# Softmax normalisation on ScalarE, and split condition blocks kept in DRAM, in a four-layer graph transformer

## The reference

```python
h = gcn(batchnorm(relu(layernorm(x))))
for i in range(4):
    q = ln(h, ln2_w[i], ln2_b[i]).reshape(16, 64, 512) @ Wq[i]     # 8 heads of 64
    k, v = cond @ Wk[i], cond @ Wv[i]                              # cond: (16, 256, 512)
    w = softmax(einsum('bnhd,bmhd->bhnm', q, k) * 64 ** -0.5)
    h = h + einsum('bhnm,bmhd->bnhd', w, v) @ Wo[i]
    u = ln(h, ln3_w[i], ln3_b[i]) @ geglu_w[i] + geglu_b[i]        # 512 -> 2 x 2048
    val, gate = split(u)
    h = h + (val * gelu(gate)) @ ffo_w[i] + ffo_b[i]
out = x + gcn(h) + relu(layernorm(x))
```

## Time and profile before

| | us |
|---|---|
| Time, median of 3 runs | 2686.38 (2684.01 to 2689.35) |
| The profiled execution's own time | 2677.4 |
| Its span, first to last instruction | 2675.6 |
| TensorE matmuls busy in it | 2401.6 (90%) |
| VectorE busy | 1936.9 (72%) |
| ScalarE busy | 1240.3 (46%) |
| GpSimd busy | 1419.8 (53%) |
| Mean granted TensorE clock | 0.962 of full speed |

### The profile page before, as it was taken

One profiled execution on the slowest core, in us unless ns is written; L12 is line 12 of the kernel. 1 busy time (PEld: TensorE's weight loads), 2 busy tenths in 40 slices (PEclk: granted clock), 3 DMA queues, 4 the chain that ended last, 5 costly groups with the idle time before them and its releaser, 6 DMA issues.

```text
span 2675.6 us, 39336 instructions
## 1 busy us (share of the span) xinstructions
PE 2401.6 (90%) x14270; PEld 2095.6 (78%) x14270; DVE 1936.9 (72%) x3287; ACT 1240.3 (46%) x2497; POOL 1419.8 (53%) x990
## 2 busy tenths in 40 slices
PE   7877888889997898889997988889997988889999
PEld 5356888878886888778886888877886888878887
DVE  9965888766566888866566888876656788876654
ACT  9933544553333545553333544553332544454322
POOL 3045765546554766546554756546555666546540
PEclk9898999999998999999998999999998999999999
DMA  2021000112111000112111000112110100112121
GB/s 71 1 112 38 33 32 32 33 40 64 55 58 41 32 33 24 40 40 63 56 62 38 33 32 17 40 32 71 56 59 32 45 20 32 40 32 71 55 96 62
DMA packets 87085, 122.29 MB, mean 46 GB/s; under 512 B 6321, under 2 KB 68401, under 8 KB 82033
## 3 DMA queue, kind: packets, MB, share of 16 engines
q1 hardware_dynamic: 86608, 115.60, 13.5%
q10 hardware_dynamic: 288, 4.19, 0.4%
HBM read 113.22 MB, written 6.55 MB: 45 GB/s over the span
## 4 chain that ended last, share of the span: by engine, by line
PE 54%; DVE 23%; POOL 8%; ACT 5%; issue 5%; DMA 4%; SPq 0%; DVEq 0%; POOLq 0%; ACTq 0%
PE ps L2265 7%; PE ps L2266 7%; PE ps L2267 7%; PE ps L2635 6%; PE ps L2639 6%; PE ps L2637 6%; PE ps L2512 3%; DMA stage<-in_condT 3%; PE ps L2515 3%; PE ps L2514 3%; DVE qbd L1945 2%; POOL cb L771 2%; POOL t_s L766 2%; DVE p_norm L1979 2%; DVE kv L1922 2%
## 5 line engine op out<-in xcount | busy, mean ns | idle before, releaser
L2512 PE MATMUL ps<-wv_hi,cb 128*128 128x256 f32 x896 | 265.4, 296 | 74.1 <-DVE kv L1907 50.7
L2512 PE MATMUL ps<-cb,wk_hi 128*128 128x256 f32 x896 | 265.1, 296 | 43.6 <-DVE kv L1922 20.1
L2514 PE MATMUL ps<-wv_lo,cb 128*128 128x256 f32 x896 | 258.6, 289 | 0.0
L2515 PE MATMUL ps<-wv_hi,cb 128*128 128x256 f32 x896 | 258.6, 289 | 0.0
L831 POOL TENSOR_TENSOR f_lo<-ff,f_hi 128x512 fp32r<-128x512 f32 x128 | 167.6, 1322 | 171.2 <-ACT f_hi L1420 171.0
L2514 PE MATMUL ps<-cb,wk_hi 128*128 128x256 f32 x896 | 258.1, 288 | 0.0
L771 POOL TENSOR_TENSOR cb<-stage,cb 128x512 fp32r<-128x512 f32 x160 | 218.2, 1375 | 74.9 <-ACT cb L980 74.9
L2515 PE MATMUL ps<-cb,wk_lo 128*128 128x256 f32 x896 | 257.4, 287 | 0.0
L2512 PEld LDWEIGHTS ps<-wv_hi,cb 128*128 128x128 f32 x896 | 177.0, 197 | 86.0 <-DVE kv L1907 56.4
L1979 DVE TENSOR_SCALAR p_norm<-p_exp,rinv 128x256 f32<-128x256 f32 x256 | 226.3, 924 | 4.7 <-DVE rinv L1976 0.2
L2200 DVE TENSOR_TENSOR h<-h,ps 128x512 f32<-128x512 f32 x256 | 169.9, 684 | 72.7 <-PE ps L2267 72.0
(11 more groups left out here) (363 smaller groups left out, 7497.5 us busy)
## 6 DMA issues: line engine op xcount, KB each, us to landing
stage<-in_pieces SPq DMA_DIRECT2D x256, 128.0 KB, 2.6
stage<-in_condT SPq DMA_DIRECT2D x32, 1024.0 KB, 4.9
stage<-in_pieces SPq DMA_DIRECT2D x44, 512.0 KB, 3.6
stage<-in_pieces SPq DMA_DIRECT2D x16, 256.0 KB, 3.2
at_s<-at_hi ACTq DMA_DIRECT2D x2, 2048.0 KB, 8.3
wq_raw<-in_pieces SPq DMA_DIRECT2D x8, 512.0 KB, 4.3
wo_raw<-in_pieces SPq DMA_DIRECT2D x8, 512.0 KB, 4.1
at_hi<-at_s SPq DMA_DIRECT2D x4, 1024.0 KB, 8.1
```

What stands on the lines that cost most here:

```text
L2512: pe.matmul(to, l_hi, r_hi, start=(fresh and i == 0 and k == 0), stop=False, skip_group_check=True)
L2514: pe.matmul(to, l_hi, r_lo, start=False, stop=False, skip_group_check=True)
L2515: last = pe.matmul(to, l_lo, r_hi, start=False, stop=(k == 1), skip_group_check=True)
```

## The change

It has four parts.

1. The two multiplications of a softmax unit move from DVE (`softmax`) to ACT (new `normalise`, an ACTIVATE with a scale per row). In the DVE queue the reciprocal moves too: behind the first `kv_late` in each unit, and ahead of `o_low`.
2. The seven split blocks of each group are made in layer 0 alone. SP writes each to DRAM (`cb_s`, 512 KB per block) as soon as its low part is done, and layers 1 to 3 load them back (`load_blocks`), a block at a time, each behind the value step that reads its predecessor in the same place. `cond_sum`, `cond_high` and `cond_low` are gone from layers 1 to 3. A KEYS step there waits for the DMA at j = 0 (four blocks) and j = 4 (three).
3. Openings: in layers 1 to 3 the weights Wv are loaded and split at the end of the layer before (loaded before the blocks, summed on DVE between the last `add_down`s). In layer 0 the raw blocks of group 0 get a place of their own, `raw0`, and are loaded earlier. `first_t2(1)` is cut in two halves around the last `q_product(0, .)`, and each transpose waits only for the copy of its own bank. `zero_q` and the splitting of q move.
4. POOL waits for the normalised tiles (`z2_ok`) ahead of the work that followed `first_rsqrt`: in the first half of the opening ahead of the splitting of Wq (and of blocks 4 to 6 in layer 0), in the second ahead of `zero_q`.

SP's loop over layers is written out in place of a loop on the engine. The core of the diff (the functions that only gained an argument `g` are left out):

```diff
@@ sync engine, start @@
-            sp.wait_ge(w_ok, 4)
-            load_raw(0)
+            sp.wait_ge(a_dec, NT)
+            sp.dma_start(flat(raw0[:, :, :]), condT[0].rearrange("p k n -> p (k n)")).then_inc(raw_in, 16)
...
+            for j in range(BLOCKS):
+                sp.wait_ge(c_lo, j + 1)
+                sp.dma_start(cb_s[0, j], cond_block_bits(j)).then_inc(cb_out, 16)
@@ sync engine, layer @@
+                def load_blocks(g, js, after):
+                    for j in js:
+                        if after is not None:
+                            sp.wait_ge(step_mm, after + j + 1)
+                        sp.dma_start(cond_block_bits(j), cb_s[g, j]).then_inc(cb_in[j // 4], 16)
...
-                with sp.Fori(2, GROUPS) as g:
-                    sp.wait_ge(c_lo, BLOCKS * GROUPS * l + BLOCKS * g)
-                    load_raw(g)
-                wait_apart(sp, c_lo, BLOCKS * GROUPS * l + BLOCKS * GROUPS)
+                if first:
+                    for g in range(1, GROUPS):
+                        for j in range(BLOCKS):
+                            sp.wait_ge(c_lo, BLOCKS * g + j + 1)
+                            sp.dma_start(cb_s[g, j], cond_block_bits(j)).then_inc(cb_out, 16)
+                        if g + 1 < GROUPS:
+                            load_raw(g + 1)
+                else:
+                    for g in range(1, GROUPS):
+                        load_blocks(g, range(BLOCKS), STEPS * kv_set(l, g - 1, VALUES))
...
                 if not last:
-                    load_raw(0)
+                    for k in range(2):
+                        sp.wait_ge(w_ok, FIRST_PIECES + PIECES * l + VALUE_PIECE[k] - 1)
+                        load_attn((pieces[base + 21], pieces[base + 25]), k, VALUE_PIECE[k] % 2)
                     wait_apart(sp, block_mm, 7 * (SETS - 1) * l + 7 * (SETS - 1))
+                    load_blocks(0, range(4), None)
                     load_whole(wq_raw, (pieces[base + 5], pieces[base + 9]))
-                    wait_apart(sp, c_lo, BLOCKS * GROUPS * l + BLOCKS * GROUPS + BLOCKS)
-                    for k in range(2):
-                        load_attn((pieces[base + 21], pieces[base + 25]), k, VALUE_PIECE[k] % 2)
+                    load_blocks(0, range(4, BLOCKS), None)
@@ gpsimd, opening of a layer @@
                 kv_low(l, 0, KEYS, 0)
                 first_rsqrt(2 * l + 1)
-                attn_low(VALUES, 0, l)
-                attn_low(VALUES, 1, l)
-                for n in range(3):
-                    cond_sum(GROUPS * l + 1, n)
+                pool.wait_ge(z2_ok, 2 * FIRST * l + 2 * FIRST)
+                if l == 0:
+                    pool.wait_ge(agg_mm, NT)
+                    pool.wait_ge(low_out, 32)
+                zero_q()
+                if l == 0:
+                    attn_low(VALUES, 0, 0)
@@ gpsimd, end of a layer @@
-                    for n in range(3):
-                        cond_sum(g, n)
-                    cond_low(g, 0)
-                    cond_sum(g, 3)
-                    for j in range(1, BLOCKS):
-                        cond_low(g, j)
+                    for k in range(2):
+                        attn_low(VALUES, k, l + 1)
                     first_rsqrt(2 * l + 2)
+                    pool.wait_ge(z2_ok, 2 * FIRST * l + 3 * FIRST)
                     for half in range(2):
                         wq_low(l + 1, half)
-                    zero_q()
@@ scalar engine @@
+                def normalise(u):
+                    act.wait_ge(rinv_ok, u + 1)
+                    for b in range(2):
+                        last = act.activation(pn[:, b, :], pe_[:, b, :], ACT.Identity, scale=rinv[:, b:b + 1])
+                    last.then_inc(pn_ok, 1)
@@ vector engine @@
                     dve.reciprocal(rinv[:, :], rsum[:, :]).then_inc(rinv_ok, 1)
-                    dve.wait_ge(rinv_ok, u + 1)
-                    for b in range(2):
-                        last = dve.tensor_scalar(pn[:, b, :], pe_[:, b, :], rinv[:, b:b + 1], None, ALU.mult)
-                    last.then_inc(pn_ok, 1)
@@ tensor engine @@
-                    if kind == KEYS:
-                        pe.wait_ge(c_lo, BLOCKS * (GROUPS * l + t) + j + 1)
+                    if kind == KEYS and l == 0:
+                        pe.wait_ge(c_lo, BLOCKS * t + j + 1)
+                    elif kind == KEYS and j in (0, 4):
+                        pe.wait_ge(cb_in[j // 4], (64, 48)[j // 4] * (GROUPS * (l - 1) + t + 1))
...
-                for p in range(PAIRS):
+                for p in range(3):
                     q_product(0, p)
-                first_t2(1)
-                for j in range(5, STEPS):
-                    kv_step(0, KEYS, j)
+                first_t2(1, range(2))
+                q_product(0, 3)
+                kv_step(0, KEYS, 5)
+                first_t2(1, range(2, KC))
+                kv_step(0, KEYS, 6)
```

200 lines of the change are left out of this document (117 added, 83 removed).

## The result

The changed kernel takes 2497.48 us, the median of 4 runs (2494.66 to 2497.91), beside 2685.22 (2684.01 to 2689.35) for the kernel before on the same chip: a ratio of 0.9296, 95% interval 0.928 to 0.9312. It is faster by 188 us; 2520 was forecast. The profiled execution took 2497.86 us, with a span of 2495.6.

What follows compares the result with a forecast made beforehand. TensorE, busy 90% of the span, was taken as the bound, so gains come from its idle or slow-clock time: 80 + 57 + 24 + 0 + 6 = 167 us off 2677.4, 2510, or 2520 against the runs' median; range 2475 to 2605.

Steps and rivals of the forecast that it cites:

- the likeliest case: Whole kernel: the summed savings arrive, time 2520 us, with a range of its own from 2485 to 2565; chance 0.63.
- the wait that was forecast at key step 6: Last unit of a group: the reciprocal, now ahead of the second `kv_late`, makes key step 6 wait 0.3 us.
- Loops of layers 1 to 3: Attention loops: TensorE's waits go, a group falls from 36.4 to 32.7 us, saving 80 us over three loops.
- The loads: Seven 512 KB block loads a group in layers 1 to 3: cost 0 while a block lands in under 8 us.
- The slower rival: Blocks land late, key step 0 waits 8.6 us in 21 groups, +181 us, time 2701; chance 0.04.
- Openings: Layers 1 to 3, first normalised tile to first `kv_two` for VALUES: 18.0 + 20.5 + 20.5, less 2, saves 57 us.
- The walk: Layer 1's opening timed step by step in the new order: 18.0 us earlier, a window of 44.3 us.
- the 5.29 us tile: Normalised tile in the old opening: its 5.29 us read as what is left of POOL's 4.94 us Wq splitting plus itself.
- Opening of layer 0: Products with Wq 10 us earlier and 13.6 us saved from there to the loop: 24 us, bounds 12 and 30.
- Loop of layer 0: Blocks still made and now stored: 0.8 us gained at step 6 against store costs a group; net 0, from -8 to +11.
- Ends of the attention stages: Last group mixed with the MLP's first products, four layers: 1.5 us of waits each goes, saving 6 us.
- ScalarE's multiplication: A softmax multiplication of 128x256 on ACT takes 0.40 us, bounds 0.344 and 0.470, covered by other work.

Runs made afterwards that it cites:

- pool_busy: Changed kernel with POOL in layers 1 to 3 doing eleven subtractions of 512 columns a group on otherwise unused SBUF tiles; 2534.7 us.
- norm_dve: Changed kernel with the two multiplications of a softmax unit back on DVE, behind the reciprocal at its new place; 2540.0 us.
- recip_late: Changed kernel with the last reciprocal of a group moved behind the second `kv_late` for KEYS, as before the change; 2487.5 us.
- late_loads: Changed kernel with each block's load in layers 1 to 3 issued three value steps later, blocks 3 to 6 all after value step 6; 2625.0 us.
- before_norm_act: Kernel before with part 1 alone, plus ScalarE's `kv_first` for KEYS ahead of the rounding of block 4; 2633.4 us, ratio 0.9819 to the kernel before.
- raw_first: Changed kernel with the next group's raw load issued ahead of the store of block 6 in layer 0; 2495.1 us.
- olow_first: Changed kernel with `o_low` ahead of the reciprocal again in the last group of each layer alone; 2484.6 us.
- busy_norm_dve: Changed kernel with both edits together: multiplications back on DVE (norm_dve) and eleven POOL subtractions a group in layers 1 to 3 (pool_busy); 2619.8 us.
- after: The changed kernel itself, with all four parts of the change; 2497.5 us.

## Why the prediction was right, and where its terms were not

The direction, the likeliest case and the range held; the forecast saving of 167 us came out as 180, and the wait that was forecast at key step 6 is in the trace with its 0.3 us. By steps:

- **Loops of layers 1 to 3: -80 forecast, -99.5 measured.** The mechanism was right (pool_busy and norm_dve bring the time back), the floor was mis-sized. I took 36.4 - 4.0 = 32.4 us for a group without waits. Measured is 31.45 (recip_late), since TensorE's own busy time also fell, from 32.38 to 31.57. A matmul behind a wait is recorded longer than its neighbours (0.36 to 0.55 us beside 0.28), so each wait removed gives back more than its length. Of the 6.5 us a loop by which I was off, this makes 4.0 in the five later groups (31.90 where I had 32.7). The other 2.5 are in the first two: group 0 takes 28.7 us where I had 29.8, and group 1, which I took for a common one, took 34.8 before and takes 31.2 now. The clock is 1.00 in all three loops, as expected.
- **The loads cost nothing.** Right: 4.5 us to landing at the median, and 7.66 us of distance for block 3 where I had 8.1. late_loads shows what lies beyond. The slower rival was underpriced: I counted its waits alone, and 86.2 us of them cost 122.9.
- **Openings: -57 forecast, -62.6 measured.** The 2 us taken off for handovers were not lost. The walk gave 44.3 us a window, measured is 43.2. The reading of the 5.29 us tile was wrong (part 4 above); the walk did not use it.
- **Opening of layer 0: -24 forecast, -21.8 measured.**
- **Loop of layer 0: 0 forecast, -5.0 measured, from two parts that were not told apart.** I gave part 1 only the 0.8 us at step 6; before_norm_act measures 12.1 us in this loop, 2.0 a group. The stores I put at 0, 1.3 or 2.6 us a group; if all of the 7.1 us is theirs, which is argued, they are 7.1 / 6 = 1.2. But their order behind the raw load is 1.7 of the 7.1 (raw_first); the load also takes longer (5.5 us at the median, 4.9 in before_norm_act).
- **Ends of the attention stages: -6 forecast, +8.9 measured. This step failed.** It took 1.5 us of the waits of the earlier trace rows off each last group without a walk through its order. There the reciprocal, moved ahead of o_low, waits for the exps while TensorE has nothing but the output product left, 3.6 us in each of the four ends where the kernel before had 2.1. The second idle stretch of an end got shorter (5.6 to 4.9 us), and two small waits (0.8 and 0.4) went, so the waiting of the four ends changed by 4 x (1.5 - 0.7 - 1.2) = -1.6 us. The time at half clock in these stretches grew from 55 to 76 us by the clock records of the two traces, which costs half of the 21 us. The estimate from these is +9 us, so the loss is the clock behind the waits, for which the sum had no term. olow_first gives 12.9 back, 5.5 of it waiting.
- **ScalarE's multiplication: 0.40 us forecast, 504 ns recorded**, above my upper bound of 0.470. Two in a row take 0.91 us, the second starting 0.40 behind the first, and TensorE never waits for them, so the miss cost nothing.

## What to carry to other kernels

When an engine's work stalls beside another's, moving the first one's work and taking away the second one's are not two separate gains: here 9.6 and 14.8 us a loop alone, 35.3 together. Walk each special group (first, last, layer 0) through the new order as carefully as the common one; the last group of four stages held 13 us that moving one call gave back, 5.5 of them waiting. An idle stretch of TensorE of 2 to 5 us is to be priced with the slow clock that may stand behind it: the 86.2 us of waits of late_loads cost 1.4 times their length, while one and the same wait of 3.6 us had 3.4 us at half clock behind it in one kernel and 6.8 in another. A gain of 5 us in such a stretch can therefore come from an edit elsewhere; look at the stretch before crediting it. And look at the mean beside the median: the stalls of busy_norm_dve hide behind a median of 354 ns.

## What was not expected of the hardware

Around the end of an idle stretch of 3.6 us TensorE's granted clock fell to 0.50, that is 1.2 GHz, for 6.8 us in after and for 3.4 in recip_late. The 21 waits of late_loads, 4.1 us in the mean, brought the granted clock of whole loops to 0.94. Beside a busy POOL a DVE operation with one input in PSUM keeps its 690 ns, while one with both in SBUF doubles or triples (680 to 1324 ns, 421 to 1212). And a normalised tile on DVE, with one SBUF input, stood still beside memsets on POOL.
